# Scattering rows half a batch ahead and starting the expert tiles before the attention stage has ended

## The chip, the cores and the metric

The kernel is one program on one core of a Trainium2 chip. The metric is the device time of that core in microseconds. The kernel before has a median of 843.71 us over three runs (842.3 to 844.35). A difference of about 0.3%, some 2.5 us, is what such measurements can tell from no change.

## The reference

A transformer layer on 16 batches of 512 tokens with 128 features, in float32. Attention (16 heads of 8, causal) and a mixture of experts (8 experts, two per token) read the same normalised input and are both added to it.

```python
x = L0_attn_x
xn = _layernorm(x, axis=-1)
x = x + _L0_attn_ref(xn, Wq, Wk, Wv, Wo) + _L0_ffn_ref(xn, Wr, W1, b1, W2, b2)
...
q = _l2norm(q); k = _l2norm(k)
sim = jnp.einsum('bhid,bhjd->bhij', q, k) * SCALE       # causal mask, softmax
o = jnp.einsum('bhij,bhjd->bhid', attn, v)
...
top_v, top_i = jax.lax.top_k(probs, K)                  # K = 2 of E = 8
for e in range(E):
    h = jax.nn.gelu(jnp.einsum('bsh,mh->bsm', x, W1[e]) + b1[e], approximate=False)
    y = jnp.einsum('bsm,hm->bsh', h, W2[e]) + b2[e]
    out = out + y * w_e[..., None]
```

## The kernel before

The program has four stages; each of the five engines runs its own instruction list, and semaphores tie them together.

**Stage one** (to about 100 us) normalises all tokens, stores them in `xn_rows` and `xn_cols`, and computes the router. For each token and each of its two experts it works out a slot in `slot_x`, a table in DRAM sorted by expert and cut into 71 tiles of 256 rows (`FFN_TILES`).

**Stage two** is attention on batches 0 to 7, one call of `body` each. A body has four quarters (`w`), each with five score units. TensorE computes scores (L769) and projections (L745) and weighs the values with the probabilities of the quarter before (L794); ScalarE takes the exponential (L677); GpSimd masks most diagonal blocks (L566, L573) and VectorE the last one (`mask2`, L1181); VectorE divides by the row sums (`divide`, `turn_divided`, L1194 to L1209) and prepares q, k and v of the next batch (`prepare`). Beside that, GpSimd scatters the rows of this batch to `slot_x`: eight indirect DMAs per batch (`move`, L555), one after each of the body's eight mask slots. Their source is a buffer of rows, filled by `load_rows` (L361) on SyncE's queue at the end of the body before. Two buffers alternate, each with a semaphore `moved[j]`.

**Stage three** is `between`: the 71 expert tiles. SyncE loads a tile of rows (`load_tile`, L419), TensorE transposes it (`turn_x`, L899) into bank 4 or 5, VectorE copies it to SBUF (`copy_x`, L1311) and copies the tile's expert weights (`copy_w1` L1297, `copy_w2` L1305), TensorE multiplies by W1 (`hidden`, L908), ScalarE applies gelu (L687), TensorE multiplies by W2 (`outputs`, L920), VectorE adds the bias (`copy_y`, L1318) and SyncE stores to `slot_y` (L423). TensorE's order is `turn_x(k+1)`, `hidden(k)`, `outputs(k-1)`. Meanwhile GpSimd scatters batches 8 to 15 without pause, as their rows come; SyncE issues the row loads of batches 10 to 15 in tiles 4, 7, 10, 13, 16 and 19, and before the load of tile 25 it waits until all rows of all batches are moved (L435). GpSimd then gathers results of the first half back (L553).

**Stage four** is attention on batches 8 to 15, with the gathers of its rows.

At the seam between stages two and three SyncE waits until every move of batches 0 to 7 has landed and then issues the loads of tiles 0, 1 and 2. TensorE does the last weighing, then waits for both halves of the division of batch 7 (`o_evac`, banks 4 and 7), then transposes tile 0. VectorE does `mask2`, `divide` and `turn_divided` for batch 7, three small operations for the gates (L1280 to L1284), and only then the weight copies and the copy of tile 0.

Of the kernel before, what the change touches and what calls it, by code (L numbers as in the profile page):

```python
# [20 lines left out]
ALU = mybir.AluOpType  # L21
# [7 lines left out]
def build(nc, x, Wq, Wk, Wv, Wo, Wr, W1, b1, W2_, b2, out):  # L29
    NB, N, D = x.shape  # L30
    E, M, _ = W1.shape
    H, DH = 16, D // 16
    TB = N // P
# [29 lines left out]
    with ExitStack() as ctx:  # L63
# [156 lines left out]
        def some(count):  # L220


            return not isinstance(count, int) or count > 0
# [6 lines left out]
        def known(i, value):  # L230

            return isinstance(i, int) and i == value
# [57 lines left out]
        def _(sp):  # L290
# [106 lines left out]

            def body(b, par, second=False, last=False):
                if not last:
                    for t in range(TB):  # L400
                        if t == TB - 1 and not (known(b, HALF - 1) or known(b, NB - 2)):
                            load_xt(b + 2)
                        turn_qk(b + 1, t, 1 - par)
                if not second:
                    if not known(b, 0):
                        load_rows(b + 1, 1 - par)
                else:
                    if not known(b, HALF):
                        count = counted_by(sp, MOVES * (b - 1))
                        sp.wait_ge(made, 1)  # L410
                        sp.wait_ge(combined, count)
                        store_out(b - HALF - 1)
                        store_out(b - 2)

            def load_tile(k, s):

                if some(k - 1):
                    sp.wait_ge(xgtr_done, k - 1)
                sp.dma_start(xg[:, s], tile_rows(slot_x, k)).then_inc(xg_in[s], 16)  # L419

# [4 lines left out]
            def between():  # L425
                for j in range(2):
                    sp.wait_ge(moved[j], 8 * MOVES * HALF)
                for k in range(3):
                    load_tile(k, k % 2)
# [34 lines left out]
        def _(pool):  # L464
# [111 lines left out]
            def body(b, par, second=False, last=False):  # L576
# [3 lines left out]
                for w in range(NQ):  # L580
                    n = NQ * b + w
                    for half in range(2):
# [11 lines left out]
                        order = [0], [1], [2], [3], [4], [5], [6], [7]  # L594
                        if known(b, 0):
                            order = [], [], [], [0, 1], [2, 3], [4, 5], [6], [7]
                        if last:
                            order = [0, 1], [2, 3], [4, 5], [6, 7], [], [], [], []
                        for o in order[slot]:
                            move(b, par, o, second)  # L600
# [98 lines left out]
        def _(pe):  # L699
# [188 lines left out]
            def between():  # L888
                weigh(HALF - 1, 1, NQ - 1, range(5))
                pe.wait_ge(o_evac, 2 * HALF)  # L890
                pe.wait_ge(proj_evac, TB * (HALF + 1))
                pe.wait_ge(added, HALF - 1)
# [20 lines left out]
                def outputs(k, s):  # L913
                    pe.wait_ge(w2_ready, k + 1)
# [28 lines left out]
        def _(dve):  # L943
# [330 lines left out]
            def between():  # L1274

                mask2(NQ * HALF - 1, NQ - 1)
                divide(HALF - 1, 1)
                turn_divided(HALF - 1)
                dve.wait_ge(gap_exp, 1)
                dve.tensor_scalar(gapx[:, 1], gapx[:, 0], 1.0, None, ALU.add).then_inc(r_step, 1)  # L1280
                dve.wait_ge(r_step, next_step())
                dve.reciprocal(gate[:, 0], gapx[:, 1]).then_inc(r_step, 1)
                dve.wait_ge(r_step, next_step())
                dve.tensor_tensor(gate[:, 1], gate[:, 0], gapx[:, 0], ALU.mult).then_inc(r_step, 1)  # L1284
                dve.wait_ge(r_step, next_step())
# [34 lines left out]

                e = copy_w1(0, 0)
                copy_w2(0, 0, e)
                copy_x(0, 0)
# [10 lines left out]
                for k in range(4):  # L1334
                    step(k, k % 2)
                with dve.Fori(2, BACK0 // 2) as i:
                    step(2 * i, 0)
                    step(2 * i + 1, 1)
# [39 lines left out]
```

## Time and profile before

| quantity | value |
|---|---|
| three timed runs | 842.3, 843.71, 844.35 us |
| the profiled execution: own time | 836.56 us |
| its span in the profile | 834.6 us |
| mean granted TensorE clock | 0.924 |
| TensorE busy | 709.8 us |
| VectorE busy | 525.5 us |
| ScalarE busy | 482.5 us |
| GpSimd busy | 437.9 us |

The profile is of one execution. Times in it count from the start of its span; around the span lie 1.96 us that it does not show. An engine's busy time is an average over stages that have different limits, so the stretches around the change have to be read by themselves. In the rows below, `start us, us` are the start and the length of a group of like instructions, `xN` their number; in brackets stands how long the engine was idle before them and what ended that. `issue` means that the engine waited for nothing that the profile shows. SPq is SyncE issuing DMAs.

### The profile page before, as it was taken

The numbers are of one execution on the slowest core, as the hardware profiler recorded it, in microseconds if no ns is written. First come the engines' busy times: TensorE is split into PE (matmuls) and PEld (weight loads), VectorE is DVE, ScalarE is ACT, GpSimd is POOL, SyncE is SP. The second block draws the span as 40 slices with busy tenths as digits, with TensorE's granted clock in tenths as the row PEclk, the third lists the DMA queues.
The fourth block names the chain that finished last, engine by engine and source line by source line (L and its number), as shares of the span: only waits on it lengthen the run. The fifth ranks groups of instructions, "written<-read, shape, count | busy, mean of one in ns | idle before, by whom it ended". The sixth has DMA issues, their size and how long they took to land. (4 is left out here: it accounts for less than half of the span.)

```text
span 834.6 us, 18970 instructions
## 1 busy us (share of the span) xinstructions
PE 709.8 (85%) x5959; PEld 438.2 (53%) x5959; DVE 525.5 (63%) x1350; ACT 482.5 (58%) x801; POOL 437.9 (52%) x558
## 2 busy tenths in 40 slices
PE   3877399999999788887899949788679999999986
PEld 2656123333333377786799939676568333333322
DVE  7699976888888623333344414443345689999964
ACT  2766368888888523332344413322234889888883
POOL 4455256777777743464300150445430777777773
PEclk9899579999999989999999969889989899999998
DMA  6886493444444544333222222222221445444441
GB/s 198 265 260 181 108 202 75 95 94 101 98 95 95 136 133 124 109 107 107 77 74 69 79 65 64 79 69 83 71 75 45 86 90 106 107 97 103 112 108 32
DMA packets 170228, 89.18 MB, mean 107 GB/s; under 512 B 77217, under 2 KB 159937, under 8 KB 170177
## 3 DMA queue, kind: packets, MB, share of 16 engines
q1 hardware_dynamic: 161984, 71.74, 34.4%
q0 software_dynamic: 8192, 16.79, 7.1%
q8 instruction: 27, 0.44, 0.2%
q14 instruction: 25, 0.20, 0.1%
HBM read 39.47 MB, written 32.24 MB: 86 GB/s over the span
## 5 line engine op out<-in xcount | busy, mean ns | idle before, releaser
L677 ACT ACTIVATE prob<-psum 128x1024 f32<-128x1024 f32 x320 | 312.6, 1027 | 60.9 <-PE psum L769 50.0
L687 ACT ACTIVATE prob<-psum,prob 128x256 f32<-128x256 f32 x284 | 116.3, 471 | 241.1 <-PE psum L908 153.2
L794 PE MATMUL psum<-prob,v 128*18 128x384 f32 (+2 forms) x2560 | 181.6, 393 | 2.7 <-DVE prob L1181 1.8
L920 PE MATMUL psum<-prob 128*128 128x128 f32 x1136 | 151.4, 287 | 30.1 <-ACT prob L687 15.8
L553 POOL DMA_INDIRECT rows<-slot_y,idx x128 | 123.8, 967 | 101.1 <-DVE acc L1234 65.0
L908 PE MATMUL psum<-xs,prob 128*128 128x256 f32 x568 | 149.8, 411 | 26.4 <-DVE xs L1311 22.7
L555 POOL DMA_INDIRECT slot_x<-rows,idx x128 | 128.4, 1003 | 76.6 <-DMA rows<-xn_rows 39.0
L920 PEld LDWEIGHTS psum<-prob 128*128 128x128 f32 x1136 | 146.6, 201 | 40.1 <-issue 17.7
L769 PE MATMUL psum<-qks 32*128 32x512 f16 (+3 forms) x1024 | 128.0, 309 | 17.7 <-DMA qks<-dup 8.1
L566 POOL TENSOR_SCALAR_AFFINE_SELECT prob<-prob 128x512 f32<-128x512 f32 x128 | 90.4, 706 | 96.0 <-ACT prob L677 95.2
L908 PEld LDWEIGHTS psum<-xs,prob 128*128 128x128 f32 x568 | 111.4, 207 | 45.6 <-issue 16.8
L769 PEld LDWEIGHTS psum<-qks 32*128 32x128 f16 x1024 | 34.0, 93 | 181.2 <-ACT prob L677 93.9
L1318 DVE TENSOR_TENSOR xs<-psum,prob 128x256 f32<-128x256 f32 x71 | 30.1, 423 | 149.4 <-remote 91.2
L794 PEld LDWEIGHTS psum<-prob,v 128*18 128x18 f32 x2560 | 54.5, 98 | 48.5 <-issue 40.5
L1297 DVE COPY prob<-wexp 128x516 f32 x71 | 31.5, 444 | 57.2 <-ACT prob L687 31.6
L1181 DVE TENSOR_TENSOR prob<-prob,causal 128x512 f32<-128x512 f32 x64 | 45.4, 710 | 30.0 <-ACT prob L677 30.0
L745 PE MATMUL psum<-wall,xt 128*128 128x384 f32 x128 | 60.0, 554 | 4.6 <-DVE v L1083 3.8
L1234 DVE SCALAR_TENSOR_TENSOR acc<-rows,gate,acc 128x128 f32 (+1 forms) x128 | 47.9, 430 | 0.0
L573 POOL TENSOR_SCALAR_AFFINE_SELECT prob<-prob 128x512 f32<-128x512 f32 x64 | 45.4, 709 | 2.9 <-ACT prob L677 2.1
L1305 DVE COPY prob<-wexp 128x640 f32 x71 | 35.2, 495 | 14.5 <-DVE xs L1318 12.2
L535 POOL COPY idx<-slots 128x8 int32 (+1 forms) x32 | 6.8, 212 | 66.8 <-DMA slot_y<-xs 66.7
L513 POOL TENSOR_TENSOR rows<-prob 128x512 f32<-128x512 f32 x16 | 20.5, 1282 | 33.9 <-DVE xns L1016 32.2
(141 smaller groups left out, 677.0 us busy)
## 6 DMA issues: line engine op xcount, KB each, us to landing
xs<-slot_x SPq DMA_DIRECT2D x71, 128.0 KB
slot_y<-xs SPq DMA_DIRECT2D x71, 128.0 KB
xs<-in_L_attn_x SPq DMA_DIRECT2D x16, 256.0 KB, 3.5
prob<-in_L_ffn_W SPq DMA_DIRECT2D x16, 256.0 KB, 3.4
xn_rows<-xns SPq DMA_DIRECT2D x16, 256.0 KB, 4.2
xn_cols<-xts SPq DMA_DIRECT2D x16, 256.0 KB, 4.2
xt<-xn_cols SPq DMA_DIRECT2D x16, 256.0 KB
rows<-xn_rows SPq DMA_DIRECT2D x16, 256.0 KB, 2.9
```

Of the source, the lines that this page charges most:

```text
L553: pool.indirect_dma_start(rows[:, j, c, t, :], None, done, where).then_inc(moved[j], 16)
L555: pool.indirect_dma_start(slot_x, where, rows[:, j, 0, t, :], None).then_inc(moved[j], 16)
L566: pool.affine_select(out=p, in_=p, compare_op=ALU.is_ge, fill=0.0, base=0, pattern=[[0, 2], [0, 2], [1, P]], channel_multiplier=-1).then_i ...
L573: pool.affine_select(out=p, in_=p, compare_op=ALU.is_ge, fill=0.0, base=0, pattern=[[0, QH], [1, P]], channel_multiplier=-1).then_inc(mask ...
L677: act.activation(prob[:, q % 2, KEPT[u], :], score[(q + u) % 2], ACT.Exp, scale=SCALE / UP ** 2).then_inc(exp_done, 1)
L687: act.activation(hs[:, s, c, :], psum[:, 2 * s + c // 2, (c % 2) * FT:(c % 2 + 1) * FT], ACT.Gelu, bias=ws[:, s, B1C + c:B1C + c + 1]).the ...
L745: pe.matmul(bank[:, 0:3 * D], xt[:, t * P:(t + 1) * P], wall[:, E:WEND], start=True, stop=True).then_inc(proj_done, 1)
L769: mm = pe.matmul(s[:, r * N + col:r * N + col + cols], qks[g:g + 32, par, 1, q, kt * P:(kt + 1) * P], qks[g:g + 32, par, 0, q, first:first ...
L794: mm = pe.matmul(ps_octet[w // 2][32 * g:32 * g + VW, first:first + cols], lhs, prob[:, w % 2, KEPT[u], c:c + cols], start=(i == 0 and not ...
L908: mm = pe.matmul(psum[:, 2 * s + c // 2, (c % 2) * FT:(c % 2 + 1) * FT], ws[:, s, c * P:(c + 1) * P], xgt[:, s, :], start=True, stop=True)
L920: mm = pe.matmul(psum[:, 6 + s, j * D:(j + 1) * D], hs[:, s, c, j * P:(j + 1) * P], ws[:, s, W2C + c * D:W2C + (c + 1) * D], start=(c == 0 ...
L1234: dve.scalar_tensor_tensor(out=a, in0=r, scalar=gate[:, c, at(TB * m + t)], in1=a, op0=ALU.mult, op1=ALU.add).then_inc(combined, 1)
```

## The change

It has three parts.

1. **Moves half a batch ahead.** In the first half a body now issues moves 4 to 7 of its own batch in slots 0 to 3 and moves 0 to 3 of the next batch in slots 4 to 7. Bodies 0, 1 and 2 build up the lead (8, 10 and 10 moves); body 7 has only four, in slots 0 to 3. `load_rows(b + 1)` goes from the end of the body to before its second transpose `turn_qk`.
2. **First tiles loaded in body 7.** Before the last `turn_qk` of body 7 SyncE waits for all moves and loads tiles 0 and 1. Tile 2 stays in `between`.
3. **Seam reordered.** VectorE copies the weights of tile 0 first, then does `mask2`, then copies tile 0; `divide` and `turn_divided` of batch 7 come after step 0, the gates (`share_gates`) after step 2. TensorE takes bank 4 once the first half is divided (`o_evac` at 15 of 16); the wait for `added` (bank 6) goes to `outputs(0)`, the wait for the second half (bank 7) to `outputs(1)`.

```diff
+            def first_tiles():
+                for j in range(2):
+                    sp.wait_ge(moved[j], 8 * MOVES * HALF)
+                for k in range(2):
+                    load_tile(k, k)
+
             def body(b, par, second=False, last=False):
                 if not last:
                     for t in range(TB):
-                        if t == TB - 1 and not (known(b, HALF - 1) or known(b, NB - 2)):
+                        if t == 1 and not second and not known(b, 0):
+                            load_rows(b + 1, 1 - par)
+                        if t == TB - 1 and known(b, HALF - 1):
+                            first_tiles()
+                        elif t == TB - 1 and not known(b, NB - 2):
                             load_xt(b + 2)
                         turn_qk(b + 1, t, 1 - par)
-                if not second:
-                    if not known(b, 0):
-                        load_rows(b + 1, 1 - par)
-                else:
+                if second:
...
             def between():
-                for j in range(2):
-                    sp.wait_ge(moved[j], 8 * MOVES * HALF)
-                for k in range(3):
-                    load_tile(k, k % 2)
+                load_tile(2, 0)
                 load_rows(HALF + 1, 1)
...
-                        order = [0], [1], [2], [3], [4], [5], [6], [7]
+                        if second:
+                            order = [0], [1], [2], [3], [4], [5], [6], [7]
+                        else:
+                            order = [4], [5], [6], [7], [8], [9], [10], [11]
                         if known(b, 0):
                             order = [], [], [], [0, 1], [2, 3], [4, 5], [6], [7]
+                        if known(b, 1):
+                            order = [0], [1], [2, 3], [4], [5], [6, 7], [8], [9]
+                        if known(b, 2):
+                            order = [2], [3], [4, 5], [6], [7], [8, 9], [10], [11]
+                        if known(b, HALF - 1):
+                            order = [4], [5], [6], [7], [], [], [], []
...
                         for o in order[slot]:
-                            move(b, par, o, second)
+                            if o < MOVES:
+                                move(b, par, o, second)
+                            else:
+                                move(b + 1, 1 - par, o - MOVES, second)
...
                 weigh(HALF - 1, 1, NQ - 1, range(5))
-                pe.wait_ge(o_evac, 2 * HALF)
+                pe.wait_ge(o_evac, 2 * HALF - 1)
                 pe.wait_ge(proj_evac, TB * (HALF + 1))
-                pe.wait_ge(added, HALF - 1)
...
                 def outputs(k, s):
+                    if known(k, 0):
+                        pe.wait_ge(added, HALF - 1)
+                    if known(k, 1):
+                        pe.wait_ge(o_evac, 2 * HALF)
...
             def between():
 
-                mask2(NQ * HALF - 1, NQ - 1)
-                divide(HALF - 1, 1)
-                turn_divided(HALF - 1)
-                dve.wait_ge(gap_exp, 1)
...
                 e = copy_w1(0, 0)
                 copy_w2(0, 0, e)
+                mask2(NQ * HALF - 1, NQ - 1)
                 copy_x(0, 0)
...
                 for k in range(4):
                     step(k, k % 2)
+                    if k == 0:
+                        divide(HALF - 1, 1)
+                        turn_divided(HALF - 1)
+                    if k == 2:
+                        share_gates()
```

## Rows read from the trace of the kernel before

**Rows 1.** Stretches: length, busy us of PE, PEld, DVE, ACT, POOL; clock, DMA share, GB/s

```profile
171.00:193.00 22.00, 21.41 (x248) 7.61 (x240) 18.08 (x39) 19.59 (x21) 16.62 (x22) 1.00 0.49 101
284.00:290.00 6.00, 1.54 (x6) 1.01 (x7) 4.77 (x13) 0.00 (x0) 4.55 (x5) 0.88 0.50 152
290.00:296.00 6.00, 6.00 (x18) 4.81 (x17) 1.09 (x3) 2.42 (x6) 4.31 (x6) 0.55 0.57 176
...
412.00:470.00 58.00, 58.00 (x404) 54.72 (x403) 26.24 (x63) 25.95 (x64) 0.00 (x0) 1.00 0.25 70
```

**Rows 2.** Timeline at the seam, TensorE

```profile
281.16 2.54 PE L794 MATMUL psum<-prob,v 128*18 128x384 f32 x40
...
283.07 0.14 PEld L794 LDWEIGHTS psum<-prob,v 128*18 128x18 f32 x8 [0.27 <-DVE prob L1181]
...
286.63 0.41 PE L899 MATMUL psum<-identf,xs 128*128 128x128 f32 x2 [2.94 <-DMA xs<-slot_x]
...
289.31 3.78 PE L908 MATMUL psum<-xs,prob 128*128 128x256 f32 x8 [1.54 <-DVE prob L1297]
...
298.06 1.89 PE L908 MATMUL psum<-xs,prob 128*128 128x256 f32 x8
```

**Rows 3.** Timeline at the seam, GpSimd's last moves and SyncE's queue

```profile
271.41 1.31 POOL L555 DMA_INDIRECT slot_x<-rows,idx  x1 [0.17 <-issue]
...
282.12 0.97 POOL L555 DMA_INDIRECT slot_x<-rows,idx  x1 [0.17 <-issue]
...
284.44 3.00 SPq L419 DMA_DIRECT2D xs<-slot_x  x3
```

**Rows 4.** Timeline at the seam, VectorE

```profile
282.32 0.69 DVE L1181 TENSOR_TENSOR prob<-prob,causal 128x512 f32<-128x512 f32 x1 [1.89 <-ACT prob L677]
...
283.77 0.72 DVE L1194 STREAM_TRANSPOSE turn<-psum 128x512 f32<-128x512 f32 x1 [0.75 <-PE psum L794]
...
285.36 0.71 DVE L1209 STREAM_TRANSPOSE turn<-turn 128x512 f32<-128x512 f32 x1
...
288.09 0.43 DVE L1297 COPY prob<-wexp 128x516 f32 x1 [1.06 <-issue]
...
288.83 0.42 DVE L1311 COPY xs<-psum 128x256 f32<-128x256 f32 x1
```

**Rows 5.** Timeline, TensorE in an undisturbed tile

```profile
415.42 1.89 PE L908 MATMUL psum<-xs,prob 128*128 128x256 f32 x8
...
417.15 1.95 PE L920 MATMUL psum<-prob 128*128 128x128 f32 x16
...
418.94 0.38 PE L899 MATMUL psum<-identf,xs 128*128 128x128 f32 x2
...
419.15 1.89 PE L908 MATMUL psum<-xs,prob 128*128 128x256 f32 x8
```

**Rows 6.** Waits of GpSimd, 284 to 412 us: us in total, times, longest

```profile
POOL slot_x L555 <- DMA rows<-xn_rows: 39.0, 6, 15.1
```

**Rows 7.** Waits of SyncE's queue, 396 to 412 us

```profile
SPq L418 <- DMA slot_x<-rows,idx: 7.3, 1, 7.3
```

**Rows 8.** TensorE's timeline in stage three, where tiles were held up

```profile
310.53 0.63 PE L899 MATMUL psum<-identf,xs 128*128 128x128 f32 x2
...
365.10 1.99 PE L908 MATMUL psum<-xs,prob 128*128 128x256 f32 x8 [2.56 <-DVE xs L1311]
...
482.37 0.38 PE L899 MATMUL psum<-identf,xs 128*128 128x128 f32 x2
...
498.30 0.65 PE L899 MATMUL psum<-identf,xs 128*128 128x128 f32 x2
```

**Rows 9.** Waits of TensorE in attention, 120 to 284 us, complete

```profile
PE psum L745 <- DVE v L1083: 2.7, 6, 0.6
PE psum L769 <- DMA qks<-dup: 2.1, 2, 1.9
PE psum L769 <- ACT prob L677: 1.3, 1, 1.3
```

More of the change, by code:

```diff
@@ L396, in store_out, with load_tile @@
                 sp.dma_start(batch_rows(out, m), acc[:, at(TB * m, TB), :]).then_inc(stored, 16)
+            def load_tile(k, s):
+                if some(k - 1):
+                    sp.wait_ge(xgtr_done, k - 1)
+                sp.dma_start(xg[:, s], tile_rows(slot_x, k)).then_inc(xg_in[s], 16)
+            def first_tiles():
[3 more added lines that the diff above has]
+                    load_tile(k, k)
             def body(b, par, second=False, last=False):
@@ L413, in body @@
                         store_out(b - 2)
[L415 to L419, printed above, removed]
             def store_tile(k, s):
@@ L1274, in between @@
             def between():
-                mask2(NQ * HALF - 1, NQ - 1)
-                divide(HALF - 1, 1)
-                turn_divided(HALF - 1)
-                dve.wait_ge(gap_exp, 1)
[L1280 to L1285, printed above, removed]
                 dve.wait_ge(b2_in, 16)
@@ L1319, in copy_y, with share_gates @@
                         .then_inc(ys_ready, 1)
+                def share_gates():
+                    dve.wait_ge(gap_exp, 1)
+                    dve.tensor_scalar(gapx[:, 1], gapx[:, 0], 1.0, None, ALU.add).then_inc(r_step, 1)
+                    dve.wait_ge(r_step, next_step())
+                    dve.reciprocal(gate[:, 0], gapx[:, 1]).then_inc(r_step, 1)
+                    dve.wait_ge(r_step, next_step())
+                    dve.tensor_tensor(gate[:, 1], gate[:, 0], gapx[:, 0], ALU.mult).then_inc(r_step, 1)
+                    dve.wait_ge(r_step, next_step())
                 e = copy_w1(0, 0)
                 copy_w2(0, 0, e)
+                mask2(NQ * HALF - 1, NQ - 1)
                 copy_x(0, 0)
```

## The prediction

> **What bounds the kernel now.** I read the page first and then the busy time by stretch, since the average hides three regimes. In an attention body TensorE is busy 21.41 of 22 us, and in tiles without disturbance 58.00 of 58 us, at a granted clock of 1.00 [rows 1]: both stages are TensorE's. At the seam between them it is busy 1.54 of 6 us [rows 1]. So a gain can only come from the seam, or from places in stage three where tiles are held up [rows 8].
>
> Next, the timeline at the seam. TensorE's last weighing starts at 281.16 and ends at 283.70, its last part released by VectorE's mask; it transposes tile 0 at 286.63, released by the tile's load, starts the first `hidden` at 289.31 and the third at 298.06 [rows 2]. Two chains fill the gap. GpSimd issues the last move at 282.12, done issuing at 283.09, and SyncE issues the first tile load at 284.44, when it has landed: 1.35 us later [rows 3]. VectorE masks from 282.32, divides and turns from 283.77 to 286.07, computes the gates, and has the first weight copy at 288.09 and the copy of tile 0 at 288.83 [rows 4]. The VectorE chain ends last, so loading tiles early would alone bring little; parts 2 and 3 of the change need each other. Then the price of slowness: `hidden(0)` takes 3.78 us where an undisturbed one takes 1.89 [rows 2, 5], and the stretch behind the gap has a granted clock of 0.55, so most of it runs at the lower of the two levels [rows 1].
>
> **Part 1, moves ahead.** It adds no instruction. Bodies 1 and 2 get ten moves each instead of eight: four extra times about 1.0 us (a move's length) and 0.3 us around it, some 5 us of GpSimd in 44 us, where it is idle 22.00 - 16.62 = 5.4 us per body [rows 1, 3]. Over all attention bodies TensorE never waits for GpSimd's masks [rows 9], body 0 with its pairs of moves included. If that slack failed, the four would cost up to 5.2 us. Below nothing, the 2.1 us that TensorE waits at body starts for transposed q and k [rows 9] could shrink, since the row load no longer stands right behind the last transpose. I take 0, the nearest row being body 0, which has pairs of moves and no such wait. On SyncE's queue the row load waits for moves of batch b-1, which now end in the middle of body b-1; behind it stand three transposes that are needed at the next body only, and its issue takes half a microsecond: nothing.
>
> **Part 2, tiles loaded in body 7.** The last move comes in slot 3. That slot's move is issued at 271.41 and takes 1.31 us [rows 3]; with 1.35 us to land SyncE passes its wait at 274.1, and tiles 0 and 1 are in ten microseconds before TensorE can use them. Queued behind that wait are the two loads and the last `turn_qk`, for batch 8, which is needed in stage four. Without this cover, with moves late by 10 us, the tiles would arrive when they do today. Tile 2 stays in `between`: its load waits for the transpose of tile 0. A load is used 286.63 - 284.44 = 2.19 us after its issue [rows 2, 3].
>
> **Part 3, the seam, step by step.** The weighing that frees the weight buffer is over by 281.16. VectorE then loads the expert's number and copies; before the copy at 288.09 it was idle 1.06 us, and the two weight copies take 288.83 - 288.09 = 0.74 us [rows 4]. So `mask2` starts at 281.16 + 1.06 + 0.74 = 282.96 instead of 282.32: the copies put 0.64 us on the path, the one cost of the order. It ends 0.69 us later [rows 4] and the weighing 0.69 us after that (283.70 - 283.01), at 284.34. TensorE transposes the loaded tile 0 in 0.41 us [rows 2], to 284.75. VectorE's copy and the start of `hidden` follow in 289.31 - 288.83 = 0.48 us [rows 2, 4]: `hidden(0)` at about 285.28 instead of 289.31, **4.0 us** earlier.
>
> From `hidden(0)` to `hidden(2)` it took 298.06 - 289.31 = 8.75 us. At full clock this is one whole tile, 419.15 - 415.42 = 3.73, one `hidden`, 417.15 - 415.42 = 1.73, and one transpose, 0.21 [rows 5]: 5.67 us, **3.1 us** less. TensorE's one gap left at the seam is about 0.5 us behind the transpose. A gap of 2.56 us in stage three was followed by a `hidden` of 1.99 us, full speed [rows 8], so I take full clock.
>
> Is anything late next? Tile 2 lands at 284.75 + 2.19 = 286.94, `hidden(0)` ends 1.73 us after 285.28, at 287.01: just in time. VectorE has after 285.2 three copies of step 0 (about 1.1 us), then `divide` and `turn_divided` (286.07 - 283.77 = 2.30), then the copies of tile 2 and its W1 (about 0.8) [rows 4]: 289.4 with both loads of the expert's number hidden, 291.5 with both exposed at 1.06 us. TensorE wants it at 285.28 + 5.67 = 290.95. That costs between 0 and 0.6 us; I take the middle, 0.3. The gates, 1 us, come after step 2, where VectorE is idle half of the time (26.24 of 58 us busy) [rows 1]. Bank 7 is wanted by `outputs(1)` only, behind `hidden(2)`: free by then. ScalarE did nothing from 284 to 290 [rows 1] and is ready.
>
> The sum at the seam: 4.0 + 3.1 - 0.3 = **6.8 us**.
>
> **Does it stay gained?** Two waits of stage three could take it back. SyncE waits 7.3 us before tile 25 for the last scattered rows [rows 7]. If GpSimd ended these when it does today, the gain would be lost there. But it waits itself, 39.0 us in six waits, for its rows [rows 6], and SyncE issues these loads by tile number; so GpSimd, and the wait before tile 25, move ahead with the tiles. Stages three and four hang on tiles as well. The shift is rigid.
>
> **The rivals.**
> *Lower clock (0.12).* TensorE falls to the lower level at the new seam too, or its first matmuls still meet the low stretch. Then only the first term remains, 4.0 us: 839.7. For it speaks today's 0.55 [rows 1], against it the 2.56 us gap without a fall [rows 8]. The Trainium skill (TensorE: Matmul & The Clock Gate, HAM oscillation) says that a kernel whose TensorE waits between groups of matmuls falls back to the throttled level at every such wait and pays the warm-up each time; today's row agrees, and by that rule what counts is whether the shorter gap is still a wait of that kind.
> *One more stall (0.16).* Tiles are held up irregularly while GpSimd moves rows back to back and not otherwise (58.00 of 58 us busy with GpSimd at 0 [rows 1]). The transpose of tile 5 should have come one tile after that of tile 4, at 298.06 + (418.94 - 415.42) + 3.73 = 305.31, and came at 310.53: 5.2 us lost under batch 9 [rows 2, 5, 8]. Batch 8's moves today fall on a TensorE that is idle or slow; tomorrow they meet tiles at full speed. One stall of that size leaves 6.8 - 5.2 = 1.6 us: 842.1.
> *The gain goes into the wait before tile 25 (0.05).* Then only GpSimd's earlier start counts, about 1.1 us (one move fewer after its last mask): 842.6. The same time would come if part 2 didn't do what it says. Against it: rows 6.
> *Slower (0.07).* Sixteen moves back to back against running tiles: in the gathers two transposes lie 498.30 - 482.37 = 15.93 us apart instead of 3.73, 12.2 us lost [rows 8]. If batches 8 and 9 come to cost that on top of today's stall, it is 12.2 - 6.8 = 5.4 us slower: 849.1. It decides from 9.3 us of added stalls on. Against it: the stall of batch 9, also at the end of sixteen moves, cost 5.2.
>
> **How the numbers follow.** The forecast (0.60) is the rigid 6.8 us. For the profiled execution: 836.56 - 6.8 = 829.8, span 827.8. That execution lies 7.15 us below the median of the timed runs, which agree within 2.1 us; the same 6.8 us off the median gives **836.9**. The stalls are irregular, so the forecast's own range is 833.5 to 839.5. The range is 833.5 to 842.7, from there over the lower clock, the one more stall and the wait before tile 25, leaving out the slower case and the tails of the forecast. What a measurement can tell from no change is 0.3%, 2.5 us: faster is forecast and lower clock, 0.72; within it are one more stall and tile 25, 0.21; slower 0.07.
>
> **What the profile after would show.** SyncE's two tile loads near 274 to 278, and the attention bodies still 22 us long with no wait for masks (part 1). First `hidden` near 285.3 and 1.9 us long, third near 291.3, clock 1.00 from 284 to 290 (part 3). VectorE's mask late by 0.6 us. GpSimd's waits for rows still six, about 39 us less what batches 8 and 9 no longer cover, and the wait before tile 25 still about 7 us. It would be wrong if `hidden(2)` is early by 7 us but tile 25 is not, if a stall stands before 300 us, or if a body grows.

## The result and the profile after

| | before | after |
|---|---|---|
| median of 20 timed runs each, taken together | 843.21 us | 846.93 us |
| after against before, 95% interval | | 1.0056 (1.0035 to 1.0076) |
| the profiled execution: own time | 836.56 us | 846.86 us |
| its span | 834.6 us | 844.8 us |
| mean granted TensorE clock | 0.924 | 0.919 |
| TensorE busy | 709.8 us | 716.5 us |

The change makes the kernel 0.6% slower. The forecast was 0.8% faster, and the measured time lies outside its range. A ratio with its interval, here and below, leaves out the times that lie more than 1.5% above the shortest of their kernel; medians are over all times. One caution for what follows: the profiled execution of before (836.56 us) was shorter than each of the 20 timed runs of the same kernel (837.03 to 846.66), so the two profiles differ by 10.3 us where the medians differ by 3.7.

The seam first. Stretches of the kernel after, to be held against [rows 1]; columns: stretch, length, busy us of PE, PEld, DVE, ACT, POOL, granted clock, DMA share, GB/s.

```profile
284.00:290.00 6.00, 5.20 (x55) 3.10 (x56) 3.74 (x8) 3.41 (x6) 4.08 (x6) 1.00 0.19 57
290.00:296.00 6.00, 6.00 (x41) 5.59 (x40) 2.46 (x6) 2.40 (x6) 4.78 (x5) 1.00 0.69 216
296.00:302.00 6.00, 3.67 (x22) 2.72 (x20) 1.68 (x4) 0.28 (x1) 4.32 (x6) 1.00 0.50 134
302.00:308.00 6.00, 3.10 (x14) 2.81 (x15) 0.00 (x0) 1.40 (x4) 4.06 (x6) 0.72 0.29 95
308.00:314.00 6.00, 2.46 (x7) 1.79 (x7) 3.39 (x9) 1.57 (x4) 0.00 (x0) 0.50 0.50 141
```

The hole at the seam is closed: 5.20 of 6 us busy at a clock of 1.00, then 6.00 of 6. A new hole stands right behind it, from 296 to 314. TensorE's timeline there, against [rows 2]:

```profile
279.00 1.16 PE L820 MATMUL psum<-wo,turn 128*128 128x128 f32 x8
...
286.90 0.66 PE L914 MATMUL psum<-identf,xs 128*128 128x128 f32 x4
287.85 1.99 PE L923 MATMUL psum<-xs,prob 128*128 128x256 f32 x8 [0.30 <-DVE xs L1320]
...
291.63 1.95 PE L939 MATMUL psum<-prob 128*128 128x128 f32 x16
...
293.63 1.89 PE L923 MATMUL psum<-xs,prob 128*128 128x256 f32 x8
295.36 1.95 PE L939 MATMUL psum<-prob 128*128 128x128 f32 x16
...
299.74 1.99 PE L923 MATMUL psum<-xs,prob 128*128 128x256 f32 x8 [2.06 <-issue]
304.09 3.10 PE L939 MATMUL psum<-prob 128*128 128x128 f32 x14 [2.35 <-issue]
308.10 0.37 PE L939 MATMUL psum<-prob 128*128 128x128 f32 x1 [0.90 <-issue]
...
308.96 0.63 PE L914 MATMUL psum<-identf,xs 128*128 128x128 f32 x2
312.71 3.78 PE L923 MATMUL psum<-xs,prob 128*128 128x256 f32 x8 [3.12 <-DVE xs L1320]
```

`hidden(0)` runs at 287.85, `hidden(2)` at 293.63, both at full speed. Then TensorE waits 2.06 us before `hidden(3)` and 2.35 us before `outputs(2)`; fourteen matmuls of `outputs(2)` take 3.10 us and the next one comes 0.90 us behind them; the wait before 312.71 ends at the lower clock (0.50 from 308 to 314). The other engines and SyncE in the same stretch:

```profile
278.24 1.04 SPq L402 DMA_DIRECT2D xs<-slot_x  x2
...
284.85 0.43 DVE L1306 COPY prob<-wexp 128x516 f32 x1 [2.20 <-issue]
...
285.60 0.68 DVE L1200 TENSOR_TENSOR prob<-prob,causal 128x512 f32<-128x512 f32 x1
...
297.46 0.42 DVE L1327 TENSOR_TENSOR xs<-psum,prob 128x256 f32<-128x256 f32 x1 [4.68 <-PE psum L939]
...
299.27 0.42 DVE L1320 COPY xs<-psum 128x256 f32<-128x256 f32 x1
308.88 0.42 DVE L1327 TENSOR_TENSOR xs<-psum,prob 128x256 f32<-128x256 f32 x1 [9.19 <-remote]
...
290.97 1.70 ACT L703 ACTIVATE prob<-psum,prob 128x256 f32<-128x256 f32 x4 [0.24 <-PE psum L923]
301.71 0.84 ACT L703 ACTIVATE prob<-psum,prob 128x256 f32<-128x256 f32 x2 [9.04 <-PE psum L923]
303.15 0.84 ACT L703 ACTIVATE prob<-psum,prob 128x256 f32<-128x256 f32 x2 [0.60 <-PE psum L923]
...
285.78 1.37 POOL L559 DMA_INDIRECT slot_x<-rows,idx  x1 [0.93 <-POOL idx L539]
...
306.11 0.96 POOL L559 DMA_INDIRECT slot_x<-rows,idx  x1 [0.30 <-issue]
```

GpSimd issues the sixteen moves of batches 8 and 9 from 285.78 to 307.07, most of them 1.27 us apart. In their second half the rest is held up. ScalarE's gelu of tile 2 waits for the first half of `hidden(2)` and for `outputs(0)`; `hidden(2)` has ended as a whole by 295.52 and `outputs(0)` before it, and the gelu starts at 301.71, 6.2 us later. VectorE's `copy_y(0)` needs `outputs(0)`, ended at 293.58, and starts at 297.46; its `copy_y(1)` needs `outputs(1)`, ended at 297.31, and starts at 308.88, just after the last move and 11.6 us later.

TensorE's two waits, marked `issue`, do have a cause in the program: `hidden(3)` waits for VectorE's copy of tile 3, which ends at 299.69 and stands behind the late `copy_y(0)`, and starts at 299.74; `outputs(2)` waits for the gelu of tile 2, which ends at 303.99, and starts at 304.09. TensorE is late mostly because the other two are. Only the pause inside `outputs(2)`, where the program waits for nothing, is its own.

In attention, the waits of TensorE from 120 to 284 us, complete, against [rows 9]; columns: who waited, for whom, us in total, times, longest.

```profile
PE psum L785 <- ACT prob L693: 7.4, 8, 1.6
PE psum L785 <- DMA qks<-dup: 0.4, 2, 0.2
PE psum L785 <- issue: 0.3, 1, 0.3
```

A wait for ScalarE's exponential that before has once (1.3 us) now stands about once in each body and sums to 7.4 us; the waits for `v` (2.7 us) are gone and those for transposed q and k are down from 2.1 to 0.4 us. The bodies grow unevenly. Of the 5.6 us that six of them are longer than before, 4.3 lie in one, from the output projection at 164.99 to that at 191.24 (26.25 us instead of 21.92): there TensorE waits 1.65 us for the exponential, and its granted clock is 0.59 from 171 to 174 and 0.50 from 174 to 177.

### The profile page after: what moved, and what is told of

Read it like the earlier page. It is cut to its first block and busy times, and to the rows that moved or that the text cites. A ratio compares the mean times of both kernels' runs of the same rounds, so it can differ in the third digit from the quotient of the medians.

```text
span 844.8 us, 18965 instructions
## 1 busy us (share of the span) xinstructions
PE 716.5 (85%) x5959; PEld 443.6 (53%) x5959; DVE 525.5 (62%) x1350; ACT 483.8 (57%) x801; POOL 439.7 (52%) x558
## 5 line engine op out<-in xcount | busy, mean ns | idle before, releaser
L939 PE MATMUL psum<-prob 128*128 128x128 f32 x1136 | 156.6, 291 | 31.1 <-ACT prob L703 15.7
L939 PEld LDWEIGHTS psum<-prob 128*128 128x128 f32 x1136 | 151.4, 206 | 42.4 <-issue 21.2
L1306 DVE COPY prob<-wexp 128x516 f32 x71 | 31.3, 441 | 55.0 <-ACT prob L703 33.8
L1200 DVE TENSOR_TENSOR prob<-prob,causal 128x512 f32<-128x512 f32 x64 | 45.7, 714 | 31.3 <-ACT prob L693 31.2
L1099 DVE TENSOR_TENSOR dup<-qn,dup 128x256 f16<-128x256 f32 x64 | 38.2, 597 | 0.0
```

The lines of the kernel that those rows point to most:

```text
L939: mm = pe.matmul(psum[:, 6 + s, j * D:(j + 1) * D], hs[:, s, c, j * P:(j + 1) * P], ws[:, s, W2C + c * D:W2C + (c + 1) * D], start=(c == 0 ...
L1200: dve.tensor_tensor(p, p, causal[:].rearrange("p (a c) -> p a c", a=1).broadcast_to([P, QH, P]), ALU.mult)\
```

## The experiments

Two readings were opposed. By the first, the moves that run ahead (part 1) cost time in the attention bodies, where I had priced them at nothing. By the second, the sixteen moves of batches 8 and 9 take the seam's gain back in stage three. Others came up on the way: the row load beside the transposes, and the time at which the row loads come.

One thing has to be known to read the numbers. The kernel before took about 758 us beside some of these kernels and about 843 us beside others, and one chip showed both. I call the first quiet and the second stalling conditions; each kernel is compared only with the kernel before taken beside it. The names come from stage three; what differs is told in the last section.

All kernels in one table. "Six bodies" is the time from the last output projection of one batch to that six batches later, tiles 3, 6 and 26 are the starts of their transposes behind the last output projection before stage three (279.00 in after), all read from TensorE's timeline of the profiled execution.

| kernel | conditions | ratio to before, 95% | median / before | six bodies | tile 3 | tile 6 | tile 26 |
|---|---|---|---|---|---|---|---|
| before | stalling | | | 131.3 | 21.6 | 39.0 | 139.0 |
| after | stalling | 1.0056 (1.0035 to 1.0076) | 846.93 / 843.21 | 136.9 | 14.4 | 40.1 | 148.6 |
| e8, changed again | stalling | 1.0033 (1.0004 to 1.0062) | 847.07 / 843.59 | 133.5 | 14.4 | 38.9 | 147.3 |
| e6, lead of two moves alone | stalling | 1.0031 (1.0005 to 1.0056) | 846.09 / 843.59 | 133.1 | 21.3 | 40.7 | 146.9 |
| e13, seam alone | stalling | 1.002 (0.999 to 1.0051) | 844.31 / 842.27 | 131.4 | 18.8 | 40.7 | 143.1 |
| e11, changed, lead of two | stalling | 0.9983 (0.9957 to 1.0009) | 843.4 / 844.76 | 133.1 | 14.9 | 37.3 | 146.2 |
| e7, e11 with row loads early | stalling | 1.0 (0.9976 to 1.0024) | 843.83 / 843.59 | 131.4 | 15.1 | 37.3 | 140.4 |
| e9, changed, moves held | stalling | one run: 858.07 / 844.76 | | 132.4 | 14.4 | 25.8 | 151.8 |
| e12, changed, paced | stalling | 0.9947 (0.9909 to 0.9985) | 842.25 / 842.27 | 132.4 | 14.4 | 27.7 | 137.3 |
| e14, lead of two, paced | stalling | 0.9934 (0.9901 to 0.9967) | 837.8 / 842.27 | 133.2 | 14.8 | 28.1 | 135.0 |
| e10, lead of two, paced | stalling | not used (see below) | 837.29 / 844.76 | 132.4 | 14.8 | 28.9 | 136.7 |
| e15, before, paced | stalling | 0.9981 (0.9949 to 1.0012) | 840.96 / 842.27 | 131.5 | 21.2 | 32.4 | 145.4 |
| before, profiled | quiet | one run: 755.11 / 757.68 | | 131.2 | 20.2 | 31.4 | 114.3 |
| e1, moves ahead alone | quiet | 1.0044 (1.0027 to 1.0062) | 760.69 / 757.98 | 133.0 | 21.0 | 32.2 | 115.3 |
| e2, seam alone | quiet | 0.9992 (0.9975 to 1.0008) | 757.3 / 757.98 | 131.2 | 18.7 | 30.2 | 113.2 |
| e3, changed again | quiet | 0.9956 (0.994 to 0.9972) | 753.94 / 757.98 | 133.2 | 14.4 | 26.1 | 108.7 |
| e4, changed, lead of two | quiet | 0.99 (0.9885 to 0.9915) | 750.02 / 757.98 | 129.1 | 14.9 | 26.3 | 110.5 |
| e5, row load early alone | quiet | 1.0002 (0.9985 to 1.0019) | 758.42 / 757.68 | 131.2 | 20.1 | 31.3 | 113.8 |

**The parts alone.** e1 is the changed kernel with the seam and the tile loads of before; e2 is before with part 3 alone.

```diff
 e1, against the changed kernel:
-                        if t == TB - 1 and known(b, HALF - 1):
-                            first_tiles()
 def between():
+    first_tiles()
     load_tile(2, 0)
...
-                mask2(NQ * HALF - 1, NQ - 1)
                 copy_x(0, 0)
 e2, against the kernel before:
-                pe.wait_ge(o_evac, 2 * HALF)
+                pe.wait_ge(o_evac, 2 * HALF - 1)
...
+                mask2(NQ * HALF - 1, NQ - 1)
                 copy_x(0, 0)
```

> Part 1 alone: moves half a batch ahead and row loads earlier, with the seam as before. Theory D (dense moves in attention): the ten moves of bodies 1 and 2 hold up the engines once, as in the changed kernel's trace, where the second and third body together lasted 5 us longer; this kernel is 3 to 6 us slower than before (ratio 1.004 to 1.007) and the trace has a gap in ScalarE and TensorE between 165 and 180 us. Theory T (the tiles meet batch 8's and 9's moves earlier): nothing in attention is at fault, ratio 1.000 within 0.002.

> Part 3 alone: the order at the seam of the changed kernel, with the moves and tile loads where they were. The first hidden then waits for the tile load, issued at 284.4 and in at 286.6, so it starts about 2 us earlier than before instead of 4, the third about 5 us earlier. Theory D: the gain stays, ratio 0.994 to 0.996. Theory T: the stalls of stage three take it back and more, ratio 1.000 to 1.008.

> The changed kernel as it is, on the same chip as the others, for a second profile. Both theories: ratio 1.004 to 1.008. What the two profiles of it share is the kernel's, what they don't is chance: if theory D holds, a stall in attention near 170 us comes again; if T holds, the time from tile 4 to tile 26 is again some 130 us, against 114 before.

e1 is 0.4% slower: part 1 costs about 2.7 us by itself. e2 shows nothing outside its interval: without early tiles the seam's order is worth 1.5 us at tile 3 (18.7 for 20.2), as the prediction said of the two parts needing each other. The changed kernel itself was 0.4% *faster* in these runs, 4.0 us by the medians. Its profile accounts for it: six bodies cost 133.2 - 131.2 = 2.0 us more, tile 26 comes 114.3 - 108.7 = 5.6 us earlier, 3.6 us net. And e3 is 760.69 - 753.94 = 6.75 us faster than e1, which lacks only parts 2 and 3: in quiet conditions the seam is worth to the end what the prediction said. Where part 1 loses is seen in VectorE's preparation of q and k. First the kernel before, quiet, then e3, both in body 1:

```profile
142.58 0.79 DVE L1076 CAST dup<-qn 128x256 f16<-128x256 f32 x1
143.29 0.28 DVE L1077 CAST dup<-qn 128x256 f16<-128x256 f32 x1
143.60 0.43 DVE L1079 TENSOR_TENSOR dup<-qn,dup 128x256 f16<-128x256 f32 x1
...
142.57 0.64 POOL L566 TENSOR_SCALAR_AFFINE_SELECT prob<-prob 128x512 f32<-128x512 f32 x1
143.38 1.04 POOL L555 DMA_INDIRECT slot_x<-rows,idx  x1 [0.17 <-issue]
```

```profile
143.07 0.79 DVE L1095 CAST dup<-qn 128x256 f16<-128x256 f32 x1
143.78 0.74 DVE L1096 CAST dup<-qn 128x256 f16<-128x256 f32 x1
144.56 0.73 DVE L1098 TENSOR_TENSOR dup<-qn,dup 128x256 f16<-128x256 f32 x1
...
143.73 0.65 POOL L577 TENSOR_SCALAR_AFFINE_SELECT prob<-prob 128x512 f32<-128x512 f32 x1
144.32 0.70 POOL L570 TENSOR_SCALAR_AFFINE_SELECT prob<-prob 128x512 f32<-128x512 f32 x1
...
145.71 1.24 SPq L377 DMA_TRANSPOSE qks<-dup  x1
...
151.05 0.39 PE L785 MATMUL psum<-qks 32*128 32x512 f16 x2 [2.14 <-DMA qks<-dup]
```

With two moves in a slot GpSimd's masks come later, and now stand beside VectorE's operations on q and k, which take 0.74 and 0.73 us instead of 0.28 and 0.43. It is the masks that slow them and not the moves: of the 28 casts like that at 143.78 between 120 and 290 us of e3, the seven beside a mask take 0.73 to 0.77 us and the other 21, 14 of them beside a move, 0.28 to 0.36; in the kernel before (quiet) and in e4 none of the 28 falls beside a mask. The last transpose is issued 1.78 us after the output projection instead of 1.0, TensorE waits 2.14 us for it, and behind the wait its granted clock is 0.57 from 151 to 154. From this body's output projection to that of the next it took 25.0 us instead of 21.8.

**A lead of two.** e4 is the changed kernel with a lead of two moves instead of four and no pairs inside a body, so that the last moves of batch 7 come in slot 5.

```diff
-order = [4], [5], [6], [7], [8], [9], [10], [11]
+order = [2], [3], [4], [5], [6], [7], [8], [9]
 known(b, 1):
-order = [0], [1], [2, 3], [4], [5], [6, 7], [8], [9]
+order = [0], [1], [2], [3], [4], [5], [6], [7, 8]
 known(b, 2):
-order = [2], [3], [4, 5], [6], [7], [8, 9], [10], [11]
+order = [1], [2], [3], [4], [5], [6], [7], [8, 9]
```

> The changed kernel with a lead of two moves in place of four: bodies 1 and 2 have nine moves each, single but for the last slot, and body 7 has six, the last in slot 5. The tiles are still in before the last weighing ends. Theory D: the stall in attention goes, 3 to 6 us faster than the changed kernel, ratio to before 0.995 to 1.001. Theory T: as the changed kernel, 1.004 to 1.008.

> The kernel before once more, for a profile on the chip of these experiments, where it takes 758 us instead of 843. Theory M (the engines are held up during dense moves on one chip and not on the other): no stalls between tile 4 and tile 24, each 3.73 us apart, and a wait at tile 25 of 6 us more than a tile. Against e1 and e3, the time from the last output projection of attention to the transpose of tile 3 is 21.0 us, as in e1.

In quiet conditions this keeps the seam's gain (tile 3 at 14.9) and turns the loss in attention into a gain of 2.1 us: 1.0% faster than before. e4 changes the length of the lead and the pairs at once, but with either lead the last four of the six bodies take 21.4 to 21.5 us each, and the difference lies in the first two, where the pairs stood (47.4 us together in e3, 43.4 in e4). So the pairs, not the lead, are what costs. I put the 0.5 us that each later body gains down to the row load that no longer stands behind the transposes, and tested that:

```diff
                     for t in range(TB):
+                        if t == 1 and not second and not known(b, 0):
+                            load_rows(b + 1, 1 - par)
```

> The kernel before with one edit: the row load of the next batch stands ahead of the second transpose of q and k instead of behind the last one. In e3 and e4 the bodies 3 to 7 last 21.4 us, in e2 21.9. Theory L: the load behind the last transpose is what costs this half microsecond at each body, so this kernel has bodies of 21.4 us and is about 3 us faster than before (0.995 to 0.998). Theory P: it is the moves' place in the body, and this kernel is as before (0.999 to 1.001).

It fell: 1.0002, and the bodies stay at 21.9 us. Why bodies with moves ahead are shorter in quiet conditions stays open.

**The stalling conditions.** From here on the kernel before took 842 to 845 us again.

e6 is e1 with the orders of e4. e7 is e4 with this edit on SyncE's list:

```diff
-if isinstance(k, int) and k % 3 == 1 and HALF + 1 + k // 3 < NB and k > 3:
-    load_rows(HALF + 1 + k // 3, (HALF + 1 + k // 3) % 2)
+if isinstance(k, int) and k % 3 == 2 and HALF + 2 + k // 3 < NB:
+    load_rows(HALF + 2 + k // 3, (HALF + 2 + k // 3) % 2)
```

> Part 1 with a lead of two moves and the seam as before: e1 without its pairs of moves in the middle of bodies 1 and 2. Theory D2 (pairs ahead of the last preparation of q and k slow VectorE's casts from 0.3 to 0.75 us, the last transposes leave later, TensorE waits 2.1 us at the next body and its clock falls; without pairs only the gain of the earlier moves stays): interval of the output projections 21.7 us in body 1 to 2 instead of 24.9, 21.4 from there on, ratio 0.996 to 0.999, against 1.0044 for e1. Theory E (the lead by itself costs, its row loads or its order): as e1, 1.003 to 1.006.

> e4 with the row loads of batches 10 to 15 two tiles earlier in stage three. GpSimd waited 8 us in all for these rows and SyncE then 10 us before the load of tile 25, so the last moves end up to 7 us earlier: the transpose of tile 25 comes 4 to 5 us after that of tile 24 instead of 9.6, and the kernel is 3 to 7 us faster than e4, ratio to before 0.981 to 0.987. If GpSimd's own rate binds, the last moves end at most as much earlier as it waited, and the gain is under 3 us.

> The changed kernel a third time, for the comparison on one more chip. Where the tiles of stage three run without stalls (before at 758 us), ratio 0.994 to 0.997 as in e3; where they stall (before at 843 us), 1.003 to 1.008 as in the first measurement. A ratio under 1 beside 843 us would mean that the first comparison was chance.

e8 repeats the loss of the first measurement. e6 shows that in these conditions the lead costs even without pairs: 1.0031. All stalling kernels with part 1 have the new wait for the exponential in attention, 2.6 to 7.4 us (2.6 in e7, 3.9 in e14, 6.8 in e6), and those without it have 0.6 to 1.3 (e13, e15, before). e7 asked whether GpSimd's waits for rows are what holds the tiles; it loads the rows of batches 10 to 15 two tiles earlier. Its forecast was written for quiet conditions and can't be held against this run; but beside the same kernel without the edit (e11, 0.9983) it gains nothing, 1.0, though its tile 26 comes 5.8 us earlier.

**What takes the seam's gain?** In e9 GpSimd starts the moves of batch 8 only when seven tiles are transposed. If the moves hold up the tiles, tiles 3 to 6 must keep their lead and the stalls come later; if the tiles stall by themselves, nothing moves.

```diff
 def between():
+    pool.wait_ge(xgtr_done, 7)
```

> The changed kernel, but GpSimd begins to scatter batches 8 to 15 only when tile 6 is transposed. In the first measurement tile 6 comes 39.0 us after the last output projection of the first half in the kernel before, and 40.1 in the changed one, though tile 3 comes at 21.6 and 14.4. Theory G (GpSimd's sixteen moves back to back hold the other engines up until they are done, whatever the tiles do, and so take the gain of the seam back): without moves tiles 3 to 6 are 3.73 us apart and tile 6 comes at 26 us. Theory H (the stall there is of the first tiles themselves, their code or their loads): tile 6 still comes at 38 to 41 us. The row loads wait for the held moves, so everything behind tile 7 is later and the kernel is slower as a whole by either. Where the tiles run without stalls anyway, tile 6 comes at 26 by both, and the run tells nothing apart.

TensorE, GpSimd and SyncE of e9:

```profile
306.31 0.38 PE L915 MATMUL psum<-identf,xs 128*128 128x128 f32 x2
...
310.68 0.44 PE L915 MATMUL psum<-identf,xs 128*128 128x128 f32 x2 [0.47 <-issue]
...
322.93 0.69 PE L915 MATMUL psum<-identf,xs 128*128 128x128 f32 x2 [7.93 <-issue]
```

```profile
308.17 1.05 POOL L559 DMA_INDIRECT slot_x<-rows,idx  x1 [0.93 <-POOL idx L539]
...
304.49 0.58 SPq L402 DMA_DIRECT2D xs<-slot_x  x1
...
319.38 0.37 SPq L361 DMA_DIRECT2D rows<-xn_rows  x1
319.80 0.51 SPq L402 DMA_DIRECT2D xs<-slot_x  x1
```

Up to the first move tiles 2 to 6 come 3.7 to 3.9 us apart, and tile 6 comes at 25.8, as in quiet conditions (26.1) and not at 38.9 to 40.1 as in the same kernel with its moves in place. So the first tiles don't stall by themselves; it is the moves that take the lead of the seam. What comes behind says less: tile 8 comes 12.25 us after tile 7, but its load (319.80) stands on SyncE's queue behind the row load of batch 10 (319.38), which waits for the held moves of batch 8. That wait is the edit's own doing and no stall of the kind looked for. Held moves end later, so the kernel as a whole loses: 858.07 us.

**Pacing.** If density is what hurts, moves of batches 8 and 9 that follow the tiles, two to a tile, should keep the gain without delaying the end:

```diff
+for j in range(2):
+    for o in range(MOVES):
+        if o % 2 == 0:
+            pool.wait_ge(xgtr_done, 4 * j + o // 2 + 1)
+        move(HALF + j, j, o, False)
```

> e4 (lead of two moves) with the moves of batches 8 and 9 paced: two for each tile transposed, over tiles 0 to 7, in place of sixteen back to back. Theory G: where tiles stall (before at 843 us), tile 6 comes at 28 to 36 us behind the last output projection in place of 40, ratio 0.991 to 0.997. Theory H: as e11. Where they don't (before at 758 us): as e4, 0.988 to 0.992.

> e4 again: the changed kernel with a lead of two moves without pairs in the middle of a body. Where tiles stall, theory G: tile 6 as in the kernel before (39 to 41 us), attention as before or 1 us longer, so the ratio is 0.999 to 1.002, while the changed kernel has 1.003 to 1.006. Where they don't: 0.988 to 0.992.

> The changed kernel with one edit: the moves of batches 8 and 9 paced, two for each of tiles 0 to 7. Theory G (the sixteen moves back to back take the seam's gain back): where tiles stall, tile 6 at 28 to 30 us behind the last output projection as in e10, against 39 to 40 in the changed kernel, and some 5 to 9 us of it kept to the end: ratio 0.992 to 0.999, against 1.003 to 1.006. The 2 to 5 us that the pairs of moves cost in attention stay. If the stalls of the later batches grow by what was saved, ratio as the changed kernel. Where tiles don't stall: as e3, 0.994 to 0.997.

> e2 again, part 3 alone, attention as before. Where tiles stall, theory G: tile 3 comes 18.7 us behind the last output projection instead of 21.6, tile 6 at 38 to 40 as before, ratio 0.999 to 1.001: the changed kernel is slower by what attention costs, not by its seam. If the earlier tiles are a cost of their own, ratio 1.003 or more.

> e10 again, since its six times lay far apart. Theory G: where tiles stall, 6 to 12 us faster than before, ratio 0.986 to 0.993; where they don't, 0.988 to 0.992.

> The kernel before with the pacing of e12 alone. Its seam still costs 21.6 us up to tile 3. Theory G: where tiles stall, tile 6 at 34 to 36 us instead of 39, 3 to 5 us faster, ratio 0.994 to 0.998, so that the difference between e12 and this kernel is the seam less the cost in attention, 2 to 5 us. Where they don't: 0.999 to 1.001.

e10's six times ran from 822.84 to 838.81 us, with one of 1259.43; its ratio of 0.9785 is not used, and e14 repeats the kernel. The 0.9947 of e12 has to be read with care too: it rests on seven of twelve times. Over all twelve the medians of e12 and before are the same (842.25 and 842.27), and the means are 840.84 and 843.00. So e12 is not shown to be faster than before, nor than e15, the kernel before with pacing (mean 840.93). Against the changed kernel without pacing it is a gain: by medians 1.004 (after and e8) comes down to 1.000, some 3.5 us, and by means over all times some 6 to 7 us. On the kernel before pacing is worth 0.2%, which its interval does not tell from nothing. With a lead of two (e14) the result is faster than before in either way of counting, 0.9934 and by medians 837.8 against 842.27, while the same kernel without pacing (e11) has 0.9983. TensorE in e12 under the same moves:

```profile
299.90 0.38 PE L919 MATMUL psum<-identf,xs 128*128 128x128 f32 x2
301.96 1.99 PE L928 MATMUL psum<-xs,prob 128*128 128x256 f32 x8 [1.67 <-issue]
...
309.49 0.38 PE L919 MATMUL psum<-identf,xs 128*128 128x128 f32 x2
```

Of the hole that was 18 us long in after, TensorE's timeline up to tile 6 keeps one wait of 1.67 us; tile 6 comes at 27.7 instead of 40.1. In e15 tile 6 comes at 32.4, 6.6 us earlier than in before, and yet the time is the same within its interval: its tile 26 comes at 145.4, beside 139.0 in the profile of before. e12 is 11.3 us ahead of before at tile 6 and 1.7 at tile 26. So a gain at tile 6 lasts to tile 26 only in part, and what takes the rest is not separated. Grouped by kernel, tile 26 comes at 135.0 to 137.3 with early tiles and pacing (e10 136.7), at 146.2 to 148.6 with early tiles without it (but 140.4 in e7), and at 139.0 to 146.9 with late tiles.

## Why the prediction was wrong, step by step

**The seam was right.** The last output projection came at 279.00 instead of 276.24, 2.8 us later. Counted from there, `mask2` starts at 282.84 by the clock of before (forecast 282.96), `hidden(0)` at 285.09 (forecast 285.28), and `hidden(2)` follows 293.63 - 287.85 = 5.78 us later (forecast 5.67). Clock 1.00, tiles 0 and 1 loaded in time at 278.24. The 0.3 us for a late tile 2 is not seen on its own: `hidden(2)` comes 0.1 us later than at full speed. Tile 3 is 7.2 us earlier behind the projection; the sum said 6.8. The rival of a lower clock is out. In quiet conditions the same two parts were worth 6.75 us to the end (e3 against e1).

**The first failed step: "The shift is rigid."** The argument was that GpSimd's rows are loaded by tile number, so that GpSimd and the wait before tile 25 move with the tiles. In quiet conditions that is what happens: the last move comes 98.9 us behind the last output projection in e3 and 104.7 in the kernel before, and the wait before tile 25 stays (9.8 and 10.0 us). In after the tiles come late, so the last move comes at 132.4 instead of 130.0, and the wait before tile 25 (7.3 us in [rows 7], forecast as about 7) is gone. What the step left out is what the moves do to the tiles when they meet. Before, the first eight of the sixteen moves fell on a seam in which TensorE was idle or at the lower clock; after, they fall on tiles at full speed. By tile 6 nothing of the 7.2 us is left, 40.1 and 38.9 against 39.0. The way from tile 3 to tile 6 takes 25.6 and 24.5 us, before 17.4, in quiet conditions 11.2 to 11.7. That the moves do this was tested by holding (e9) and by pacing them (e10, e12, e14); how they do it stays open, and so does whether it is GpSimd's work or the transfers that it starts. The rival "one more stall" described exactly this meeting and priced it at 5.2 us; it measured 7.1 to 8.2 between tile 3 and tile 6. [rows 8] had shown the place (a stall under batch 9), and the rival got 0.16 against 0.60 for a shift that no row supported. Two of the signs that the prediction named for being wrong came: a stall before 300 us, and bodies that grow.

**The second failed step: part 1 at nothing.** The row on which I took 0, that TensorE never waits for GpSimd's masks, holds after the change as well. The cost came by ways that it doesn't cover. In quiet conditions pairs of moves push GpSimd's masks beside VectorE's work on q and k: 2.0 us over six bodies, gone with the pairs (e4). In stalling conditions six bodies take 132.4 to 136.9 us with part 1 (131.4 in e7) and 131.3 to 131.5 without. TensorE's waits for the exponential grow there, from 1.3 to 7.4 us in after, while its other waits shrink from 4.8 to 0.7; so all of them together account for some 2 of the 5.6 us, and the rest is not laid out beyond the stretch at the lower clock. Part 1 alone measured 2.7 us (e1) and, with a lead of two, 2.5 us (e6). The bounds I had written, -2.1 to 5.2, hold it; the value taken from body 0 didn't. Body 0 has its pairs in slots 3 to 5 and no move at all in slots 0 to 2; bodies 1 and 2 have moves in every slot.

**The sum in its place.** Seam -7.2, meeting of moves and tiles +7.1 to +8.2, part 1 +2.5 or more: some 3 us slower, measured 3.7. This sum ends at tile 6 and takes the rest as equal, so that it comes out so close is in part luck. Whole times say the same, more coarsely: in stalling conditions the seam adds nothing that can be told (e13 alone 1.002; e8, with the longer lead, 1.0 us slower than e6 by medians), and part 1 alone costs 2.5 us. In quiet conditions the middle term is missing, and the result is a gain of 4.0. The slower rival asked for 9.3 us of added stalls from sixteen moves; it had the right place, but with part 1's cost beside it less was enough. What is not separated: how much of the loss behind tile 6 belongs to the change. After and e8 need 108.6 and 108.4 us from tile 6 to 26, before 100.0, e6 106.2, e13 102.4, e15 113.0, one profile each.

**The base.** The profile of before came from an uncommonly short execution. Reading its stalls as the typical ones made tile 26 look earlier (139.0) than in kernels with the same seam (145.4 in e15, 146.9 in e6).

## What to carry to other kernels

A gain ahead of a stage is kept only if nothing in that stage holds it up: look at what the engine that isn't the bound does in the stretch into which the work moves, and price the meeting, not the shift. Work added to GpSimd also shifts what GpSimd does behind it: here two moves in a row put its masks beside VectorE's critical operations, and that cost more than the moves' own length. When a background stream holds the tiles up, tie it to the progress of the tiles with a wait; here that one edit took back the loss of the change, and with a lead of two moves it gave a gain. When an engine waits and the profile names nobody, read the program's own waits first: three of the long ones here had a cause in another engine or queue.

## What the runs showed of the hardware

**Stalls without a cause in the trace, in two conditions.** The same kernel took 758 us or 843 us, steadily within a set of runs, and the same chip gave both. Two stretches of stage three of the kernel before, first in stalling, then in quiet conditions:

```profile
300.00:330.00 30.00, 25.67 (x164) 23.12 (x162) 10.20 (x24) 9.73 (x24) 11.57 (x14) 0.94 0.52 149
330.00:360.00 30.00, 24.21 (x148) 21.43 (x148) 9.97 (x24) 9.79 (x24) 14.01 (x17) 0.94 0.34 98
```

```profile
300.00:330.00 30.00, 29.57 (x207) 27.60 (x206) 13.23 (x31) 13.07 (x32) 16.45 (x19) 1.00 0.59 168
330.00:360.00 30.00, 30.00 (x210) 28.36 (x209) 14.39 (x33) 13.20 (x32) 19.98 (x23) 1.00 0.49 142
```

In the quiet runs GpSimd moves more rows in the same time (16.45 and 19.98 us busy) and TensorE still has 29.57 and 30.00 of 30 us. So dense moves alone don't make stalls; in the other condition the stalls of tiles 3 to 6 need them (e9). Tiles 3 to 26 take 94.0 us quiet and 117.4 stalling, tiles 44 to the last, with the gathers, 97.5 and 152.3; tiles 26 to 44, where GpSimd is nearly idle (5.9 of 67.2 us busy), take 67.2 in every profile of both. The single moves that the kernel before has in attention cost no more in one than in the other: six bodies take 131.3 and 131.2 us. What switches the condition stays open; nothing here could set it.

**VectorE is not the only one held.** The Trainium skill (SBUF — State Buffer, SBUF: two separate sides) says that within the engine side only the port pair shared by VectorE and GpSimd contends, and that PE, ACT and VectorE's own pair never wait for anyone. The casts beside masks (0.73 to 0.77 us instead of 0.28) agree. The stalls don't fit it: ScalarE starts a gelu 6.2 us after its last operand, and TensorE pauses where the program has no wait. The two transposes of one tile in e8, which stand side by side in the list and are one group of 0.38 us elsewhere:

```profile
405.94 0.27 PE L914 MATMUL psum<-identf,xs 128*128 128x128 f32 x1
407.26 0.37 PE L914 MATMUL psum<-identf,xs 128*128 128x128 f32 x1 [1.05 <-issue]
```

By the page such a hold lasts for one instruction of the other engine; here the gelu is late by the length of some five moves. The traces don't tell whether these engines themselves are held or the signals between them.
